# Four heads' products together in four row groups of TensorE, and VectorE's mask product in its scalar form

## What is computed

```python
Q = (x @ Wq.T).reshape(b, n, H, DH).transpose(0, 2, 1, 3)      # H = 8 heads of DH = 32
K = (x @ Wk.T).reshape(b, n, H, DH).transpose(0, 2, 1, 3)
V = (x @ Wv.T).reshape(b, n, H, DH).transpose(0, 2, 1, 3)
scores = jnp.einsum('bhnd,bhmd->bhnm', Q, K) / jnp.sqrt(jnp.float32(DH))
scores = jnp.where(adj[:, None, :, :] == 0, -jnp.inf, scores)
attn = jax.nn.softmax(scores, axis=-1)
out = jnp.einsum('bhnm,bhmd->bhnd', attn, V)
out = out.transpose(0, 2, 1, 3).reshape(b, n, H * DH)
return out @ Wo.T + bo
```

## Time and profile before

| | |
|---|---|
| median of 3 runs | 3994.09 us (3990.95 to 3995.72) |
| span of the profiled execution | 3982.8 us |
| median less that span | 11.3 us |
| PE (TensorE) busy | 3709.5 us, 93% of the span |
| DVE (VectorE) busy | 3101.9 us, 78% |
| ACT (ScalarE) busy | 1994.8 us, 50% |
| POOL (GpSimd) busy | 1576.2 us, 40% |

### The profile page before, as it was taken

The page is one execution under the profiler, slowest core; times in us unless marked ns, Lnnn a source line. Parts: engine busy times, 40 slices in busy tenths (PEclk is TensorE's granted clock), DMA queues, the critical chain, the costliest instruction groups (busy, mean ns, idle before and its releaser), DMA issues.

```text
span 3982.8 us, 59433 instructions
## 1 busy us (share of the span) xinstructions
PE 3709.5 (93%) x19042; PEld 2707.6 (68%) x19042; DVE 3101.9 (78%) x5637; ACT 1994.8 (50%) x3047; POOL 1576.2 (40%) x980
## 2 busy tenths in 40 slices
PE   7999579999999999999999999999999999999986
PEld 6888346676667766666666676766677666666665
DVE  6787557888887888888888888888878888888752
ACT  4656145555555555555545545555555555555430
POOL 4667234333443444444433333334434444444310
PEclk9999689999999999999999999999999999999986
DMA  8988322222222212222222222222222212222200
GB/s 286 317 310 298 93 53 64 70 69 69 63 58 69 60 52 56 53 69 69 69 69 69 69 69 69 69 69 63 58 69 59 58 52 53 69 69 69 53 16 11
DMA packets 195935, 341.10 MB, mean 86 GB/s; under 512 B 28720, under 2 KB 64432, under 8 KB 195888
## 3 DMA queue, kind: packets, MB, share of 16 engines
q1 hardware_dynamic: 195888, 340.50, 30.3%
HBM read 188.89 MB, written 50.33 MB: 60 GB/s over the span
## 4 chain that ended last, share of the span: by engine, by line
PE 78%; DVE 10%; ACT 4%; issue 3%; POOL 2%; DMA 2%; SPq 1%; DVEq 0%; ACTq 0%; POOLq 0%
PE bank L1444 12%; PE bank L1495 12%; PE obank L1378 12%; PE bank L1233 9%; PE pair L1233 7%; PE pair L1362 7%; PE bank L1406 6%; PE bank L1463 3%; PE pair L1339 3%; DVE minus_max L1033 2%; PE obank L1265 2%; DMA pT<-in_adjT 2%; PE bank L1265 1%; DVE b_st L841 1%; ACT hsq L632 1%
## 5 line engine op out<-in xcount | busy, mean ns | idle before, releaser
L602 POOL TENSOR_TENSOR pT<-pT,node_edge 128x1024 f32<-128x1024 f32 x256 | 628.6, 2462 | 532.0 <-ACT pT L690 530.1
L690 ACT ACTIVATE pT<-pair 128x1024 f32<-128x1024 f32 x512 | 515.9, 1031 | 325.6 <-PE obank L1378 248.2
L1033 DVE TENSOR_REDUCE minus_max<-pair 128x2 f32<-128x1024 f32 x512 | 603.3, 1216 | 56.9 <-PE pair L1339 56.5
L1023 DVE TENSOR_TENSOR pT<-pT,node_edge 128x1024 f32<-128x1024 f32 x256 | 399.8, 1562 | 269.4 <-ACT pT L690 266.2
L1495 PEld LDWEIGHTS bank<-v,p3T 128*128 128x128 f32 x4096 | 502.4, 199 | 36.2 <-DVE p3T L1182 24.5
L1495 PE MATMUL bank<-v,p3T 128*128 128x65 f32 x4096 | 499.8, 280 | 20.2 <-DVE p3T L1182 20.2
L540 POOL TENSOR_TENSOR d_rs<-d_ve,minus_half 128x4 f32<-128x4 f32 x32 | 32.2, 1007 | 1207.5 <-DVE d_ve L853 1207.5
L1378 PE MATMUL obank<-pT,v 128*64 128x512 f32 x2048 | 490.3, 611 | 8.4 <-POOL pT L602 4.8
L1444 PE MATMUL bank<-w_s,hid 128*128 128x256 f32 x2048 | 479.6, 389 | 0.3 <-DVE hid L1112 0.3
L1444 PEld LDWEIGHTS bank<-w_s,hid 128*128 128x128 f32 x2048 | 383.6, 192 | 87.7 <-issue 40.1
L632 ACT ACTIVATE p3T<-x,d_sh,d_rs 128x256 f32<-128x256 f32 x128 | 66.4, 589 | 720.6 <-POOL d_sh L546 720.6
(11 more groups left out here) (189 smaller groups left out, 6468.7 us busy)
## 6 DMA issues: line engine op xcount, KB each, us to landing
pT<-in_adjT SPq DMA_DIRECT2D x64, 512.0 KB, 5.3
a_at<-in_adjT SPq DMA_DIRECT2D x64, 512.0 KB, 3.6
q_parts<-high_parts SPq DMA_DIRECT2D x256, 128.0 KB, 4.7
k_parts<-high_parts SPq DMA_DIRECT2D x256, 128.0 KB, 4.1
b_at<-in_adjT SPq DMA_DIRECT2D x64, 512.0 KB, 3.9
hid<-in_x SPq DMA_DIRECT2D x32, 512.0 KB, 4.4
x_res<-hid SPq DMA_DIRECT2D x32, 512.0 KB, 5.0
pre_bn<-hsq SPq DMA_DIRECT2D x32, 512.0 KB, 4.1
```

Of the source, the lines that this page charges most:

```text
L602: nc.gpsimd.tensor_tensor(half, half, node_edge[:, 0:2, :], ALU.mult).then_inc(a_masked[0].sem, 1)
L690: nc.scalar.activation(dst, pair[p][:, :, :], func, **more).then_inc(a_copied[p].sem, 1)
L1023: nc.vector.tensor_tensor(half, half, node_edge[:, 2:4, :], ALU.mult).then_inc(a_masked[1].sem, 1)
L1033: nc.vector.tensor_reduce(minus_max[:, t, 2 * two_heads:2 * two_heads + 2], pair[p][:, :, :], AX.X, ALU.max, negate=True).then_inc(a_copie ...
```

## The change

The eight steps of TensorE are now `a.nat{j}`, each with four matmuls into both buffers: heads 0 and 1 of a chunk of 128 rows into pair0, heads 2 and 3 into pair1. They read four different groups of 32 rows. Before, both buffers of a step held the same two heads (one pair of row groups) for two node tiles. A step now waits for both buffers before its first matmul. VectorE's reductions keep their places and write the columns of minus_max that belong to the new contents. VectorE's half of the mask product becomes scalar_tensor_tensor with a factor of 1.0.

```diff
@@ ORDER (one place)
-a.nat50:0 h.head1:3 p.vc:1 b.norm3:3 b.ms:2 a.vmask5:1 a.nat51:0 b.flip30:2 b.sumsq5:2 a.nat60:0 h.prob2:3 b.sumsq6:2
-b.flip31:2 a.div0:1 b.diag:2 a.nat61:0 b.e:2 a.vmask6:1 a.nat70:0 b.sumsq7:2 b.scale0:2 b.scale1:2 a.vmask7:1
+a.nat4:0 b.tanh3:3 p.khigh:1 h.prob1:3 a.wo1:1 a.vmask4:1 a.nat5:0 h.head1:3 p.vc:1 b.norm3:3 b.ms:2 a.vmask5:1
+b.flip30:2 b.sumsq5:2 a.nat6:0 h.prob2:3 b.sumsq6:2 b.flip31:2 a.div0:1 b.diag:2 b.e:2 a.vmask6:1 a.nat7:0 b.sumsq7:2
@@ VectorE
-                    nc.vector.tensor_tensor(half, half, node_edge[:, 2:4, :], ALU.mult).then_inc(a_masked[1].sem, 1)
+                    nc.vector.scalar_tensor_tensor(out=half, in0=half, scalar=1.0, in1=node_edge[:, 2:4, :], op0=ALU.mult,
+                                                   op1=ALU.mult).then_inc(a_masked[1].sem, 1)
-            def a_max(h, q):
-                two_heads, t = divmod(2 * h + q, T)
+            def a_max(j, p):
+                chunk, t = divmod(j, T)
+                two_heads = 2 * chunk + p
@@ TensorE
-            def a_nat(h, q):
-                two_heads, t = divmod(2 * h + q, T)
+            def a_nat(j):
+                chunk, t = divmod(j, T)
 
                 def f(g):
 
                     pe.wait_ge(*a_high_ok.upto(g, 2))
-                    dst, full = a_free(g, U_NAT + 2 * h + q)
-                    for b in range(2):
-                        chunk, r = divmod((2 * two_heads + b) * DH1, P)
-                        i = nc.tensor.matmul(dst[:, b, :], q_high[r:r + DH1, chunk, t * P:(t + 1) * P],
-                                             k_high[r:r + DH1, chunk, :], start=True, stop=True)
-                    i.then_inc(full, 1)
+                    into = [a_free(g, U_NAT + 2 * j + p) for p in range(2)]
+                    for p, (dst, full) in enumerate(into):
+                        for b in range(2):
+                            r = (2 * p + b) * DH1
+                            i = nc.tensor.matmul(dst[:, b, :], q_high[r:r + DH1, chunk, t * P:(t + 1) * P],
+                                                 k_high[r:r + DH1, chunk, :], start=True, stop=True)
+                        i.then_inc(full, 1)
                 return f
```

More of the change, by code:

```diff
@@ L79 @@
 p.k0:0 p.k1:0 p.x1:0 b.sumsq3:2 b.v3c1:3 a.vmask0:1 h.values30:3 a.headc2:2 p.v0:0 a.exp71:2 p.flipc:1 a.mask3:1
-b.sumsq4:2 b.tanh0:3 p.v1:0 h.values31:3 b.tanh1:3 a.load0:0 a.nat00:0 a.nat01:0 b.out20:2 a.nat10:0 a.headc3:2
-a.vmask1:1 p.qhigh:1 a.nat11:0 b.tanh2:3 b.out21:2 h.prob0:3 a.vmask2:1 h.head0:3 a.nat20:0 a.nat21:0 b.out22:2
-a.nat30:0 a.nat31:0 a.vmask3:1 b.out23:2 a.wo0:1 a.nat40:0 b.tanh3:3 a.nat41:0 p.khigh:1 h.prob1:3 a.wo1:1 a.vmask4:1
-a.nat50:0 h.head1:3 p.vc:1 b.norm3:3 b.ms:2 a.vmask5:1 a.nat51:0 b.flip30:2 b.sumsq5:2 a.nat60:0 h.prob2:3 b.sumsq6:2
-b.flip31:2 a.div0:1 b.diag:2 a.nat61:0 b.e:2 a.vmask6:1 a.nat70:0 b.sumsq7:2 b.scale0:2 b.scale1:2 a.vmask7:1
[L85 to L89, removed]
+b.sumsq4:2 b.tanh0:3 p.v1:0 h.values31:3 b.tanh1:3 a.load0:0 a.nat0:0 b.out20:2 a.nat1:0 a.headc3:2 a.vmask1:1
+p.qhigh:1 b.tanh2:3 b.out21:2 h.prob0:3 a.vmask2:1 h.head0:3 a.nat2:0 b.out22:2 a.nat3:0 a.vmask3:1 b.out23:2 a.wo0:1
+a.nat4:0 b.tanh3:3 p.khigh:1 h.prob1:3 a.wo1:1 a.vmask4:1 a.nat5:0 h.head1:3 p.vc:1 b.norm3:3 b.ms:2 a.vmask5:1
+b.flip30:2 b.sumsq5:2 a.nat6:0 h.prob2:3 b.sumsq6:2 b.flip31:2 a.div0:1 b.diag:2 b.e:2 a.vmask6:1 a.nat7:0 b.sumsq7:2
+b.scale0:2 b.scale1:2 a.vmask7:1 h.head2:3 p.flipl:0 b.scale2:2 b.flip3c0:3 h.prob3:3 b.agg0:1 b.flip3c1:3 a.mask4:1
+a.shift:0 b.silu0:2 b.silu1:2 b.scale3:2 b.vt:2 b.agg1:1 b.norm:2 b.v30:2 p.qlow:0 b.hid0:1 b.hid1:1 a.scores00:0
+b.load:1 h.store:3 b.silu2:2 b.silu3:2 b.exps:3 p.klow:0 a.scores01:0 b.hid2:1 b.aggc0:2 a.div1:1 a.mask5:1 a.load1:0
+b.v31:2 a.scores10:0 a.shiftc:1 p.rstd:0 a.max00:0 a.max01:0 b.edges:2 b.aggc1:2 a.max10:0 b.hidc0:2 p.sortq:0
+a.edges0:0 h.head3:3
 """.split()
@@ L1022, in f @@
                     half = pT[:, h % 2, 2:4]
-                    nc.vector.tensor_tensor(half, half, node_edge[:, 2:4, :], ALU.mult).then_inc(a_masked[1].sem, 1)
-                return f
-            def a_max(h, q):
-                two_heads, t = divmod(2 * h + q, T)
+                    nc.vector.scalar_tensor_tensor(out=half, in0=half, scalar=1.0, in1=node_edge[:, 2:4, :], op0=ALU.mult,
+                                                   op1=ALU.mult).then_inc(a_masked[1].sem, 1)
+                return f
+            def a_max(j, p):
+                chunk, t = divmod(j, T)
+                two_heads = 2 * chunk + p
                 def f(g):
-                    p, n = a_unit(U_NAT + 2 * h + q)
+                    _, n = a_unit(U_NAT + 2 * j + p)
                     dve.wait_ge(*a_filled[p].upto(g, n + 1))
@@ L1205, in _ @@
                 "p.qlow": a_low(0, U_Q, q_high, q_low), "p.klow": a_low(1, U_K, k_high, k_low), **{f"a.xmid{q}": a_wo(q) for q in range(2)},
-                **{f"a.max{h}{q}": a_max(h, q) for h in heads1 for q in halves},
+                **{f"a.max{j}{p}": a_max(j, p) for j in range(K * T) for p in range(2)},
                 **{f"a.vmask{h}": a_mask(h) for h in heads1}, **{f"a.div{k}": a_div(k) for k in range(K)},
@@ L1505, in _ @@
                 **{f"p.v{q}": a_v(q) for q in halves}, **{f"a.wo{q}": a_wo(q) for q in halves},
-                **{f"a.nat{h}{q}": a_nat(h, q) for h in heads1 for q in halves},
+                **{f"a.nat{j}": a_nat(j) for j in range(K * T)},
                 **{f"a.scores{h}{q}": a_scores(h, q) for h in heads1 for q in halves},
```

## The result

The changed kernel takes 4021.68 us (4019.61 to 4025.32), the kernel before 3993.76 beside it: 1.0069 times as long, 95% interval 1.0055 to 1.0083. It is slower by 28 us; I had forecast 4000 with a range up to 4011.

What follows compares the result with a forecast made beforehand. TensorE bounds most of a graph, VectorE the stretch around steps 5 and 6, and lost clock adds 1.16 us per graph. 3994.1 - 25 (shorter steps) + 22 (clock) + 9 (first graphs) = 4000 us, range 3976 to 4011.

Steps and rivals of the forecast that it cites:

- the gain of 25 us: Shorter steps in the stretch bound by TensorE save 0.83 us in each of 30 graphs, 25 us in all.
- the clock's share of 22 us: Lower TensorE clock behind longer waits takes back most of the 0.83 us per graph, 22 us in the sum.
- the 9 us of the first graphs: Waiting for both buffers costs the first two graphs 7 and 2 us, where VectorE's reductions set the pace; bounds 5 and 11.
- I take 0.33: A step's four matmuls in four row groups run together in 0.33 us instead of 0.66; bounds 0.33 and 0.66.
- Sum 0.83 us per graph: Steps 0 to 3, in the stretch bound by TensorE, together save 0.83 us per graph, after step 2's wait.
- steps 4 and 5 lie in front of waits: nothing: Steps 4 and 5 stand ahead of TensorE's waits, so their shorter matmuls gain nothing.
- in a graph with full clock costs nothing: Step 6, moved ahead of the transposes, delays line 1471, which still ends in time for VectorE with 0.6 us to spare.
- It takes back the upper end, 0.73: Lost clock takes back 0.45 to 0.73 of the 0.83 us per graph; the upper end was taken, leaving 0.1.
- the third rival: "Slower": every graph loses clock over line 1471, mean 1.2 us against 0.83 gained, 4014 us with the first graphs; chance 0.15.
- So one such gap does it at some times and not at others: A 1.48 us TensorE wait before line 1391 is followed by half clock in one graph, by 2.4 GHz in another.
- The scalar form, nothing: The mask product in scalar form changes the time by 0, bounds -3 and +3 us; TensorE does not wait for it.
- The same 11.3 us lie around it after the change: The profiled execution's span, 3982.8 us, is 11.3 below the median; the same difference was expected after the change.

Runs made afterwards that it cites:

- run 5: Changed kernel plus thirteen spare matmuls (results unread) per graph: five before the second output product, six before step 6, two before the bilinear terms; 3959.6 us, 0.991.
- run 11: Kernel before plus eleven spare matmuls per graph, in waits at the second output product, steps 6 and 7 and the aggregation; 3961.08 us, 0.9922.
- run 12: Run 3's kernel plus twelve spare matmuls per graph, in each wait that is left; 3944.09 us, 0.9878.
- run 3: Kernel before with only the four row groups; each pair waits for its own buffer, order as before; 3987.19 us, 0.9989.
- run 4: Changed kernel with step 6 moved back behind the second group of transposes; 4001.38 us, 1.0026.
- run 8: Run 3's kernel with only the second pair of step 6 moved ahead of the second transposes, no joint wait; 4006.01 us, 1.0027.
- run 9: Changed kernel, but its first two graphs wait for each buffer by itself; 4009.35 us, 1.0042.
- run 1: Kernel before with only VectorE's mask product in its scalar form; 3992.77 us, 1.0002.
- run 2: Changed kernel, joint waits and place of step 6 kept, but each step multiplies two heads for two node tiles as before; 4103.18 us, 1.028.
- run 6: Kernel before plus six spare matmuls per graph: five before the second output product, one before step 6's first pair; 3992.97 us, 0.9999.

## Why the prediction was wrong

Two terms of the sum failed: the gain of 25 us, which measured 7, and the clock's share of 22 us, which measured 26; the 9 us of the first graphs were 10. So -25 + 22 + 9 became about -7 + 26 + 10. The steady graphs, split with runs 5, 11 and 12, whose clock is 1.00 (us per graph):

| | at full clock | lost clock | mean |
|---|---|---|---|
| before (run 11) | 104.67 | 1.14 | 105.81 |
| four row groups, run 3 (run 12) | 104.23 | 1.54 | 105.77 |
| changed (run 5) | 104.42 | 2.08 | 106.50 |

- **"I take 0.33" for a step: wrong, 0.43 us.** The four do start together, but the row of before showed only two. The error was to take the bound on the favourable side where nothing showed four. The Trainium skill, "TensorE: Matmul & The Clock Gate", Part 3, states 3.07 times for four row tiles, from which the prediction worked out an estimate of 0.43 us and 16 us in all; the trace agrees with the 0.43.
- **"Sum 0.83 us per graph": wrong, 0.25** (104.67 - 104.42), the largest error of the forecast. Each step saves 0.22 to 0.23 us, and step 2's wait takes back part, as forecast: the stretch ends 0.45 earlier (line 1393's first group starts 2583.78 - 2567.00 = 16.78 us into its graph, line 1391's 2658.10 - 2640.87 = 17.23 before). The joint wait is not what costs there: run 12 waits by buffer and ends the stretch as early (16.80), since its second pair waits for the same reduction. Then "steps 4 and 5 lie in front of waits: nothing" fails: step 5 too waits for a second reduction (0.36 us) and starts 23.17 us into its graph (2590.17 - 2567.00), as it did before (2664.05 - 2640.87 = 23.18, row below). So VectorE comes to the reductions of step 5 later: 23.72 us into its graph in run 5 (2552.85 - 2529.13), 23.55 in run 12 (2955.47 - 2931.92), which has no joint wait, 23.98 before. From them it runs without a gap to the line 1142, and the 0.17 us are still there at the aggregation. Of the 0.44 us a graph of the changed kernel keeps 0.25. That makes 28 x 0.25 = 7 us, where the forecast counted 25 for 30 graphs.

Timeline of TensorE in the kernel before, the end of the bound stretch and step 5 in the graph of rows 2:

```profile
2658.10 1.89 PE L1391 MATMUL obank<-wo_s,att1T 128*128 128x256 f32 x8
...
2664.05 0.93 PE L1339 MATMUL pair<-high_parts 32*128 32x512 f32 x4
```

- **Step 6 "in a graph with full clock costs nothing": right.** Run 5 has the moved step and the wait in front of it, at 104.42 us a graph.
- **"It takes back the upper end, 0.73": right in kind and direction, low in size: 0.94** (2.08 - 1.14), 26 us for 28 graphs. The graph without loss is gone, as the forecast said; in the place of a pattern of four, all graphs lose clock over line 1473, and most over the transposes ahead of it too. That is the third rival, to which I gave 0.15. Runs 4 and 8 put 18 to 19 us on the move of the step; run 5 shows that it acts through the clock alone. "So one such gap does it at some times and not at others" was read rightly from the gap of 1.48 us; behind the new one, forecast at 1.9 us and measured at 1.49 to 2.05, low clock stands in all 28 graphs.
- **The first two graphs, "+9": 10.0 by run 9.** The hand-overs cost more than 0.9 us: the steps come 3.33 us apart (488.42 - 485.09), where two pairs took 2 x (0.34 + 0.79) = 2.26 us before, 1.07 more each.
- **The scalar form, nothing: right** (run 1). The comparison with line 977 was of a mean with a single shape's time: the median of the mask products is 1226 ns before and in run 1 and 1225 in the changed kernel, and the means of 1562 come from long ones of up to 3.0 us. So most mask products already took what line 977 takes.
- **"The same 11.3 us lie around it after the change": wrong.** The changed kernel's profiled execution took 4022.53 us around a span of 4020.7. The 11.3 us were not around the span: the profiled execution of before was itself shorter than the median, for the most part in its set-up. VectorE's line 917 (916 in the changed kernel) started at 410.23 us in it, and at 413.8 to 418.1 in runs 2 to 4 and the changed kernel, whose code up to there is the same. That is 4 to 8 us; the rest may lie in the graphs, so 105.81 and the lost clock of 1.14 are from an execution that was shorter than most. The sum was made against the median, so this moved nothing in it.

The two sums agree: 28 x (106.50 - 105.81) = 19.4 us and 10.0 at the start make 29, measured 27.9. Taken one after the other: row groups -5.6 (run 3), the moved step +17.7 (run 8 against run 3), the joint waits +15.8 (the rest), of which 10.0 at the start. Run 4 against run 3, joint waits without the moved step, gives 14.2 for them (8.6 + 5.6). But the parts hang together: without the row groups, the joint waits and the moved step cost 110 us (run 2), and what does that isn't shown.

## What to carry to other kernels

A wait that costs nothing by the timeline may cost TensorE its clock, and the price then stands in other lines: before a change moves work out of a wait, look at what the granted clock is behind that wait in each repetition. When the mean of repetitions exceeds the one with full clock, fill the waits with spare matmuls: it tells in one run what the clock costs, and here it also gave the fastest kernel. Too few can do nothing: in run 6 six of them in two waits only moved the loss to the waits behind. And where one wait on two buffers replaces two waits, list for every place, the first repetitions too, which reduction each buffer waits for.

## What the hardware showed beyond the forecast

- TensorE went to 1.2 GHz behind the wait ahead of step 6 (1.49 to 2.05 us) in each of the 28 graphs of the changed kernel, behind waits of 1.48 us in some graphs of before and not in others, and in run 6 behind three of 0.57 to 0.72 us close together, which the graph of rows 2 has too (0.57, 0.73 and 0.62 us) without losing the clock. With 11 to 13 products of some 0.25 us in a graph of 104 us, placed in such waits, the granted clock of the 28 graphs was 1.00, and the kernel took 30 us less (run 11), 43 (run 12 against run 3) and 62 (run 5).
- The mean graph was 105.77 to 105.84 us in four kernels of different work: before, with run 6's spare products (2962.54 / 28), with the row groups (run 3) and with run 4's order (2963.47 / 28). With the row groups and with run 4's order, what a graph saved at full clock came back as lost clock. Each mean is from one execution, and the executions of the kernel before alone differ by up to 10 us (3988.12 to 3998.73), 0.3 us a graph if it lay in the graphs; so the agreement may be closer than it would be again. Why it levels out was not tried.
